# A post-norm attention and mixture-of-experts block on one Trainium2 core: another hand-written order of the attention steps on all five queues

## The reference, cut to what matters

```python
def _L0_attn_ref(x, W_in, b_in, W_out, b_out):      # x: 4 x 1024 x 256, H = 16 heads of 64
    proj = x @ W_in.T + b_in
    q, k, v = ...                                   # b h t 64
    q, k = _rope(q, sin, cos), _rope(k, sin, cos)
    att = einsum('bhqd,bhkd->bhqk', q, k) / sqrt(64)
    att = where(tril, att, -inf)
    att = softmax(att, axis=-1)
    y = einsum('bhqk,bhkd->bhqd', att, v)
    return y.transpose(0, 2, 1, 3).reshape(b, t, H * 64) @ W_out.T + b_out

x = _layernorm(x + attn(x))
x = _layernorm(x + ffn(x))                          # 16 experts, the top 3 of each token
```

## Time and profile before

| | us |
|---|---|
| median of 3 runs | 1947.05 |
| the profiled execution | 1947.0 |
| its span, first to last instruction | 1945.0 |
| PE busy | 1733.5 (89%) |
| DVE busy | 1407.3 (72%) |
| POOL busy | 1178.5 (61%) |
| ACT busy | 761.3 (39%) |

### The profile page before, as it was taken

One profiled execution on the slowest core, in us unless ns is written; L12 is line 12 of the kernel. 1 busy time (PEld: TensorE's weight loads), 2 busy tenths in 40 slices (PEclk: granted clock), 3 DMA queues, 4 the chain that ended last, 5 costly groups with the idle time before them and its releaser, 6 DMA issues. The chain is left out here.

```text
span 1945.0 us, 33742 instructions
## 1 busy us (share of the span) xinstructions
PE 1733.5 (89%) x9679; PEld 1293.7 (67%) x9681; DVE 1407.3 (72%) x3369; ACT 761.3 (39%) x1691; POOL 1178.5 (61%) x1084
## 2 busy tenths in 40 slices
PE   5489999999999999999999999946779999999930
PEld 4357667667667667667767667523459999999930
DVE  3368888888888888888888888745974444444448
ACT  3134444454444444444444444416442222222226
POOL 2247777677677677678678678450335555555544
PEclk9689999999999999999999999978559999999975
DMA  9766457557567566557566556149002222222255
GB/s 316 260 192 188 143 172 212 153 172 208 156 177 209 153 180 202 158 174 202 167 171 202 149 166 182 34 158 370 15 20 71 70 70 70 70 70 70 70 187 184
DMA packets 164513, 300.97 MB, mean 155 GB/s; under 512 B 18768, under 2 KB 57360, under 8 KB 163360
## 3 DMA queue, kind: packets, MB, share of 16 engines
q1 hardware_dynamic: 152608, 269.79, 46.6%
q0 software_dynamic: 10752, 29.37, 4.8%
q10 hardware_dynamic: 1024, 0.26, 0.1%
HBM read 192.15 MB, written 106.95 MB: 154 GB/s over the span
## 5 line engine op out<-in xcount | busy, mean ns | idle before, releaser
L675 ACT ACTIVATE prob<-b_ps 128x512 f32<-128x512 f32 (+3 forms) x768 | 353.1, 488 | 361.6 <-PE b_ps L520 254.2
L447 POOL TENSOR_TENSOR acc<-acc,prob 128x1024 f32<-128x1024 f32 (+1 forms) x192 | 352.3, 1835 | 6.5 <-ACT prob L675 4.1
L420 POOL TENSOR_TENSOR roped<-rot 128x512 f32<-128x512 f32 x128 | 174.4, 1363 | 208.8 <-DVE rot L763 208.0
L519 PE MATMUL b_ps<-q,k 128*128 128x512 f32 (+3 forms) x768 | 294.8, 388 | 4.0 <-DMA q<-mrow 2.7
L512 PE MATMUL a_ps<-k,q 128*128 128x512 f32 (+3 forms) x768 | 264.9, 381 | 20.4 <-DMA k<-scratch_hilo 11.1
L745 DVE CUSTOM_DVE_ANT_0 masked<-a_ps,causal 128x128 bf16<-128x128 f32 (+3 forms) x512 | 237.8, 480 | 55.0 <-PE a_ps L512 45.5
L593 PE MATMUL y_ps<-prob,v_sb 128*64 128x512 f32 (+3 forms) x1536 | 273.8, 491 | 0.0
L520 PE MATMUL b_ps<-q,k 65*128 65x512 f32 (+3 forms) x768 | 264.0, 348 | 0.0
L1405 DVE TENSOR_SCALAR hT<-h_ps,b1T 128x128 f32<-128x128 f32 x448 | 126.1, 344 | 184.2 <-PE h_ps L1324 183.8
L789 DVE RECIPROCAL inv<-inv 128x128 f32<-128x128 f32 x256 | 232.2, 929 | 8.7 <-ACT inv L707 6.3
L425 POOL TENSOR_TENSOR lo<-roped,hi 128x512 fp32r<-128x512 f32 x128 | 177.5, 1387 | 83.9 <-ACT hi L688 83.9
(11 more groups left out here) (246 smaller groups left out, 2568.5 us busy)
## 6 DMA issues: line engine op xcount, KB each, us to landing
q<-scratch_hilo SPq DMA_DIRECT2D x192, 256.0 KB, 4.5
k<-scratch_hilo SPq DMA_DIRECT2D x192, 256.0 KB, 5.2
scratch_hilo<-hi SPq DMA_DIRECT2D x64, 512.0 KB, 4.1
scratch_hilo<-lo SPq DMA_DIRECT2D x64, 512.0 KB, 4.7
w_sb<-scratch_wsplit SPq DMA_DIRECT2D x32, 512.0 KB, 3.6
w<-in_L_ffn_W_dram SPq DMA_DIRECT2D x32, 512.0 KB, 10.3
got<-scratch_ys SPq DMA_DIRECT2D x32, 384.0 KB, 6.9
wv_sb<-scratch_wsplit SPq DMA_DIRECT2D x16, 512.0 KB, 6.2
```

The costliest lines, as they stand in the source:

```text
L447: nc.gpsimd.tensor_tensor(sums, old, probs(q), ALU.add).then_inc(m["sum_p"], 1)
L519: nc.tensor.matmul(out, k1[s][:, h, js], q1[s][:, h, qs], start=True, stop=False, skip_group_check=True)
L675: nc.scalar.activation(probs(q)[:, h, :], b_ps[:, h, 0:w], ACT.Exp).then_inc(exp_done[h], 1)
```

## The change

Four tables are reordered (PE, ACT, DVE, POOL), and SP's as well. Every event of the old tables is in the new ones once per step, with the same waits. On PE the value products and sums stood in three unbroken groups per step (D1 V8 V9 V10 V11; V0 V1 V2 D0 V3; V4 V5 V6 V7) and now stand in four (V10 V11 D1 V0 V1 V2; V3 D0 V4; V5 V6 V7; V8 V9). O0 moves from the end of its step to the start of the next. Seven lines of tables change:

```diff
--- before.py
+++ after.py
@@ -33,17 +33,17 @@
     return [(w.rstrip("+-"), w.count("+") - w.count("-")) for w in text.split()]
 
 
-PE_ORDER = parse("""B0.0 A0.0+ B0.1 A0.1+ A1.0+ B1.0 A1.1+ A2.0+ B1.1 X1 B2.0 A2.1+ A3.0+ B2.1 F0++ B3.0 A3.1+ D1- V8- V9- V10-
-V11- B3.1 B4.0 A4+ B4.1 F1++ A5.0+ B5.0 V0 V1 V2 D0 V3 B5.1 B6.0 A5.1+ O1- A6.0+ B6.1 B7.0 X0+ A6.1+ B7.1
-A7.0+ B8.0 V4 V5 V6 V7 B8.1 A7.1+ B9.0 O2- B9.1 B10.0 A8.0+ F2++ A8.1+ B10.1 A9.0+ O3- B11 A9.1+ A10.0+ O0
-A10.1+ A11.0+ F3++ A11.1+""")
-ACT_ORDER = parse("""E0.0 E0.1 E1.0 E1.1 E2.0 w1 E2.1 E3.0 d1- h0++ N1- E3.1 E4.0 E4.1 h1++ E5.0 d0 h2++ E5.1 E6.0 N0 E6.1 E7.0
-w0+ E8.0 E7.1 h3++ E8.1 E9.0 E9.1 E10.0 v2++ E10.1 E11.0 E11.1 v3++""")
-DVE_ORDER = parse("""M11.1 M0.0+ C0 M0.1+ M1.0+ M1.1+ M2.0+ k0 M2.1+ M3.0+ k1 k2 r0++ M3.1+ R4- r1++ R5- M4.1+ k3 M4.0+ R6- R7-
-M5.0+ r2++ G1- r3++ M5.1+ o1- M6.0+ R0 M6.1+ R1 M7.0+ R2 R3 G0 M7.1+ o2- M8.0+ M8.1+ M9.0+ o3- M9.1+ M10.0+
-o0 M10.1+ M11.0+""")
-POOL_ORDER = parse("""K11- T0 T1 T2 a0++ l0++ T3 a1++ l1++ a2++ l2++ K5 a3++ K6 l3++ K7 T8 T9 K8 T10 K9 T11 K10""")
-SP_ORDER = parse("""L1+ S3+ L0++ W0++ S0++ W1++ S1++ S2++""")
+PE_ORDER = parse("""B0.0 A0.0+ O0- B0.1 A0.1+ B1.0 A1.0+ X1 A1.1+ B1.1 A2.0+ B2.0 A2.1+ F0++ B2.1 A3+ B3 V10- V11- D1- V0 V1 V2
+B4.0 A4.0+ B4.1 O1- B5.0 A4.1+ A5.0+ F1++ B5.1 A5.1+ B6.0 A6.0+ V3 D0 V4 B6.1 A6.1+ B7.0 A7.0+ B7.1 V5 V6 V7
+A7.1+ X0+ B8.0 A8.0+ B8.1 A8.1+ F2++ B9 O2- A9.0+ F3++ B10.0 A9.1+ A10.0+ O3- A10.1+ B10.1 B11.0 A11.0+ V8 V9
+A11.1+ B11.1""")
+ACT_ORDER = parse("""E11.1- E0.0 E0.1 E1.0 w1 E1.1 E2.0 E2.1 E3.0 E3.1 N1- h0++ d1- E4.0 E4.1 h1++ E5.0 E5.1 E6.0 N0 d0 E6.1 E7.0
+h2++ E7.1 w0+ E8.0 E8.1 v2++ E9.0 h3++ E9.1 v3++ E10.0 E10.1 E11.0""")
+DVE_ORDER = parse("""C0 M0.0+ o0- M0.1+ M1.0+ M1.1+ M2.0+ M2.1+ k0 k1 r0++ M3.0+ k2 M3.1+ r1++ k3 R4- M4.0+ R5- o1- M5.0+ R6- M4.1+
+R7- r2++ M5.1+ M6.0+ G1- R0 M6.1+ M7.0+ R1 r3++ R2 M7.1+ R3 M8.1+ M8.0+ G0 o2- M9.0+ M9.1+ M10.0+ o3- M10.1+
+M11.0+ M11.1+""")
+POOL_ORDER = parse("""K10- T11- K11- T0 T1 T2 a0++ T3 l0++ a1++ l1++ K5 a2++ K6 l2++ K7 a3++ T8 K8 T9 l3++ K9 T10""")
+SP_ORDER = parse("""S2+ S3+ W0++ L0++ S0++ S1++ L1++ W1++""")
 
 UNITS = 12
 ON_DIAGONAL = (0, 1, 2, 3, 8, 9, 10, 11)
```

## The result

The changed kernel takes 1969.38 us (median of 4 executions, 1965.56 to 1973.22); the kernel before took 1948.51 us beside it (4 executions). The ratio is 1.0102, with a 95% interval of 1.0075 to 1.0129: slower by 1%, where 1947.0 was forecast with a range to 1958. The profiled execution took 1967.45 us.

A forecast was written before the change was run, and what follows sets the result against it. PE was taken to bound the step, as a sum of distances between matmul starts. The terms, 0.35 - 0.20 - 0.28 + 0.13 = 0.00 a step, times 31, left 1947.0 us, range 1938 to 1958.

The forecast's parts named there:

- Term 1: Fourth group of value products, V8 with V9, on PE: its ways in and out cost +0.35 us a step.
- Term 2: O0, moved behind the next step's A0.0, no longer waits for o3 to empty the shared bank: -0.20 us a step.
- Term 3: Start of a step, B0.0 to F0: waits of 0.21 to 0.22 in place of 0.50, -0.28 us a step.
- Term 4: V0 and V4 wait for copies N1 and N0: +0.13 us a step, between zero and 0.2 each.
- S2, bounded at 0 to 2 us in all: Stacked load S2 lands at 9.6, A4.0 needs it at 11.6; steps loading x may lose 0 to 2 us in all.
- At zero: Places expected to cost nothing, such as B7.1's wait for E6.1, the same before and after.
- The drains decide: Rival at A1.1 behind M0.1: o0 0.3 later, the start wins nothing, 0.28 a step, 1956 us; chance 0.27.
- The waits cost nothing: Rival: Term 3 and Term 4 lose their waits of 0.22 and 0.13, -0.35 a step, 1936 us; chance 0.28.
- S2 lands late: Rival: S2 lands over 2 us later than forecast; 0.5 more in every step gives 1962 us; chance 0.04.

The follow-up runs named there:

- run 4: The changed kernel with V8 and V9 put back ahead of V10 and V11, so three groups a step: 1971.81 us, ratio 1.0107.
- run 7: The kernel before with only O0 moved behind the next step's A0.0 and o0 behind C0: 1972.19 us, ratio 1.0124.
- run 5: The changed kernel with the cut T11 ahead of the sum K10 on GpSimd: 1963.83 us, ratio 1.0075.
- run 2: The changed kernel with TensorE's wait for the copy N placed behind its wait for v, before V0 and V4: 1963.89 us, ratio 1.0068.
- run 3: The changed kernel with V4 moved from behind D0 to ahead of V5: 1962.88 us, ratio 1.0071.
- run 6: The changed kernel with l3 moved behind T8, no longer behind T9, on GpSimd: 1968.64 us (three executions), ratio 1.0105.
- run 8: The changed kernel with the edits of run 2, run 5 and run 6 together: 1960.24 us, ratio 1.0052.
- run 9: Run 8 with the store W1 and then the load S2 ahead of the loads L1 on SyncE's queue: 1948.18 us, ratio 1.0006.
- run 1: The changed kernel with the store W1 ahead of the loads L1 on SyncE's queue: 1967.01 us, ratio 1.0086.
- run 10: Run 9 with V4 moved from behind D0 to ahead of V5: 1944.67 us, ratio 0.9979.
- run 11: Run 7 with V8 and V9 as a fourth group behind A10.0, where O0 was: 1985.78 us, ratio 1.0187.

## Why the prediction was wrong

It said that the terms cancel to 0.00 a step. Measured in ordinary steps, they come to 0.35 - 0.20 - 0.14 + 0.49 = 0.50, and the step is 0.45 longer; the 0.05 between could not be placed. By its own steps:

- **Term 1, +0.35: right.** The ways in and out of V8, V9 are those of the earlier trace rows, 0.34. What it lacked is that the group also covers a wait: without it PE loses more (run 4). The Trainium skill, "TensorEngine Tiling (Array Packing)", Key Properties, says that a change of tiling mode drains TensorE; the gaps of 0.09 and 0.11 agree, and the rule leaves open whether TensorE would have stood at that place anyway.
- **Term 2, -0.20: right here, wrong as a separable term.** O0 has no wait any more. Moved alone it costs 0.87 a step (run 7), since it had covered a wait for maxima. In the changed order V8 and V9 cover one at the end of the step (run 4).
- **Term 3, -0.28: too good by 0.14.** It let C0 take its time of before. K10, which before ran beside M11.1 and M0.0, now runs beside C0, and C0 takes 0.93 us and not 0.23; o0 starts 1.90 after B0.0 and not 1.66, and X1 waits. With K10 out of the way F0 starts at 3.93 (run 5), where the term's own sum has 3.89: its reckoning of TensorE and VectorE held, and GpSimd was left out of it. Run 5 shows the cause, runs 2, 3 and 6 that it sets the start of the step: C0 ends 0.02 to 0.03 behind K10 in each. The Trainium skill, "SBUF — State Buffer", Who interferes with whom, says that a VectorE instruction with two inputs in SBUF contends with a GpSimd instruction that reads SBUF, that the contention is an exclusive lock, and that the order of issue decides who is blocked. The rows agree (K10 starts first, and C0 takes 0.93 us in place of 0.22), and the rule would have spoken against this change.
- **Term 4, +0.13: the step that failed most.** V0 costs 0.23 and V4 0.26 where 0.065 each was put down, 0.49 in all; that is 0.36 a step too little, 11 us of the 20. "The load follows 0.05 later" was the wrong step: it follows 0.22 later, half of it because a second, fulfilled wait is walked through behind the one that was late (run 2). The prediction named 0.2 each as an upper bound, but for another reason, an exponential in ACT's way, and that did not occur: N1 and N0 started in time.
- **S2, bounded at 0 to 2 us in all: 9.1 in the profiled execution, and 5.8 to 12.0 in those of runs 2 to 6 and 8.** The prediction had the landing at 9.6 and A4.0 at 11.6; the trace has the last part of k for it at 9.3 to 12.1 in ordinary steps and A4.0 at 12.4. So no ordinary step waits, as it said, but the cover is 0.3 to 3.1 and not a steady 2. The x-load steps were mis-sized: the load of x takes 7 us in step 5 and the store behind it lands 3.9 us later than in step 16 (43.6 against 39.7). The bound was put down without working out that step. Run 9 shows that the late steps go when the data are early and the store and S2 are both ahead of the load of x; run 1 (the store ahead alone) and run 6 (early alone) each left some.
- **At zero:** B7.1 held (0.14 in both kernels). The prologue won 4.0 us, not lost up to 2, and step 0 won 2.5; the stretch behind the last step was 3.9 longer, on which nothing was said, and which is within what other executions show. No term gave a reason for the 6.5 us won up to step 1: that the total is not further off is luck.
- **The rivals.** "The drains decide" had the sign, 0.28 of the 0.45 of an ordinary step, and a part of the reason: o0 did come late, by 0.24, but through C0 and GpSimd. "The waits cost nothing" was wrong, and "S2 lands late", held to be 4% likely and meant for every step, came true in three steps out of 31.

Beyond the terms the sum itself was the wrong model. It took PE's time as a sum of distances that can be changed one by one. In fact two other chains touch it: VectorE's maxima at the end of a step, where O0 or V8 and V9 fill the wait, and GpSimd's 19.9 us from K5 to K10 with hardly a pause, which meets it at X1 through C0. What is won on PE between them is lost again until the meeting point is moved (V4: 0.26 won and 0.23 lost in run 3, 0.15 won and kept in run 10).

**Open:** why the transfers of S2 are slower beside the load of x (only their landings were seen), why run 9's step is 0.07 longer than run 8's, what holds steps 6 and 14 up a second time, what of run 11's loss a new order of ACT would give back, and what makes the stretches ahead of step 0 and behind step 31 differ. These were not tried.

## What to carry to other kernels

A piece of work in a hand-made order has two prices, what it costs and what it covers; take it out of its place on paper and look at who waited behind it before calling the end of its own wait a gain. When a wait on the bounding engine goes and the time stays, look for the chain on another engine that is as long as the period, and find where the two meet: here an operation of 0.2 us on 8 columns that was stretched to end with a GpSimd sum. And put the semaphore wait that will be late last.

## What the runs showed of the hardware

- **The order of waits has a price.** With a fulfilled wait behind the late one the weight load goes out 0.219 us behind the copy's end, with the late one last 0.113 us (medians of 19 steps of each, in front of V0 and of V4 alike).
- **VectorE and GpSimd hold each other up on two-input operations out of SBUF, both ways.** In lines from 300 to 1200 us the sum of 128x512 on VectorE (k2) takes 692 ns before and, beside `a0`, 1393 after; the product G, 955 before and 1730 after:

```profile
L793 DVE TENSOR_TENSOR yT<-yT,inv 128x512 f32<-128x512 f32 x48 | 83.0, 1730 | 0.0
L783 DVE TENSOR_TENSOR acc<-acc,prob 128x512 f32<-128x512 f32 x24 | 33.4, 1393 | 0.0
```

  These rows are of the changed kernel. C0 went from 230 ns to 930, and k3 the other way, from 1133 to 410, since no sum of GpSimd starts ahead of it any more. GpSimd is held too: in these rows of the changed kernel the sum a2 on GpSimd takes 1.75 us beside a G on VectorE, where a0 and a3 take 1.28.

```profile
728.12 1.97 DVE L793 TENSOR_TENSOR yT<-yT,inv 128x512 f32<-128x512 f32 x1
729.49 1.75 POOL L420 TENSOR_TENSOR roped<-rot 128x512 f32<-128x512 f32 x1
```

  The operation o0, which reads PSUM and SBUF, took 0.69 us with K10 beside it (run 5) and 0.68 in the changed kernel, where K10 had ended. Most of VectorE's 1.9 us a step more comes from here, and of all these only C0 was seen to hold TensorE up. Run 5 shows it by an experiment for C0; for the others it is read from what ran beside them.
- **A load of x of 7 to 9 us makes the transfers beside it late.** In the changed kernel the store W1 landed 3.7 to 5.7 us after its issue in ordinary steps and 7.3 to 8.3 behind the load of x, in run 6 up to 10.5. The last of the four loads of S2 took 5.1 us in step 16 and 8.5 beside the load of x in run 1.
